# Four of twelve query units ahead of a loop with a run-time trip count, in a one-core graph, attention and experts kernel

## The chip, the cores and the metric

The kernel runs as one program on one core of a Trainium2 chip. The metric is the device time of one execution in microseconds (us). The time before is the median of three runs, 812.83 us, with 811.21 us the lowest and 817.26 us the highest. The profile is of a fourth execution.

## The reference, cut to what matters

```python
xn = layernorm(x)                      # 1250 nodes x 512
x = x + gnn(xn, edges) + mix(xn)       # this stage
x = x + ffn(layernorm(x))              # shared and routed experts, later

# gnn: mean over the incoming edges (40000 edges, sorted by target)
agg = segment_sum(xn[src], dst) / max(count, 1)
h = relu(layernorm(xn @ w_self.T + agg @ w_neigh.T + bias))

# mix: linear attention, 8 heads of 64
phi(t) = elu(t @ proj) + 1
kv = phi(k).T @ v;  z = 1 / (phi(q) @ phi(k).sum(0))
out = (phi(q) @ kv * z) @ w_proj + b_proj
```

The change touches phi(q) and the mean over the edges. With the projection folded into the weights, phi of a value u is relu(u) + exp(-relu(-u)): two Relu's and one Exp on ScalarE, and one addition on VectorE.

## The kernel before, in words

Nodes are held in ten tiles of 125. Every engine has its order of work written out by hand, and all hand over through semaphores. Around the change the order is this.

**Ahead of the loop.** VectorE makes one-hot matrices of the edges, TensorE multiplies them into counts (L1284), ScalarE copies the counts out (L490), and TensorE multiplies them with the normalized rows (`spread`, L1291). Nine of the ten blocks of nodes are done so at fixed places, with the key and value products (L1228) and their sum over nodes (`kvacc`, L1309) between them. The last of these on TensorE are `spread`, `degrees` and `kvacc(9)`. ScalarE ends this part with `aggregate_out(8)` (L497).

**The loop.** What is left is done in a loop whose trip count is read at run time from `tab` by each engine (`value_load`, L1370 on TensorE). For this data it is passed once: five one-hot pairs on VectorE (L812, L815), 40 count matmuls (L1284), three copies on ScalarE (L540), 20 matmuls of `spread` (L1291) and ten of L1379, which set `x_mm`. Four of the five one-hot pairs are made before TensorE comes to the loop; the fifth waits for TensorE's first count in it.

**The means.** VectorE adds the loop's result (L911), inverts the counts and scales the ten blocks of `aggacc` (L920, each sets `an_rdy`). `means_T(b)` then turns block b: four transposes on TensorE (L1387) into bank 6 or 7, a copy to 16 bit on ScalarE (L545, `aT_h`) and the low part on VectorE (L924, `aT_rdy`), which frees the bank for block b + 2.

**The query units.** There are twelve, in order n = 0 to 11: eight of 500 nodes and four of 250. Unit n is 12 matmuls on TensorE (`split3`, L1228, called from L1397) into a bank `qb[n % 4]`, then Relu, Relu, Exp on ScalarE (L558, L559, L561) into a place of `mscr`, then the addition into `qphi` on VectorE (L935, `q_rdy`). There are two places, so ScalarE's unit n waits for `q_rdy` of unit n - 2. `qphi` lies over `aggacc`, so no addition can be made before all means are turned; on VectorE all ten low parts stand ahead of the first addition. On TensorE the means are laid between the units by `MEANS`: 0, 1, 2 after unit 0; 3, 4, 5 after unit 1; 6, 7 after unit 2; 8, 9 after unit 3. On ScalarE means 0 to 2 stand after unit 0 and 3 to 9 after unit 1. Units 4 and later wait on TensorE for the Relu's of unit n - 4 (`q_rel`).

**Among them** `unit(1)` and `unit(2)` convert weights from `stg` to `W`: one activation on ScalarE (L427) and one operation on VectorE (L714, `w_rdy`). They stand after query units 4 and 8 on both engines. SyncE loads weight unit u into `stg` when `w_rdy` has reached u - 1 (L267, L268). VectorE also copies the key-value sums into `kvbd` after its second addition (L946, L947).

**The attention.** Over ten tiles t: `att(t)` on TensorE (L1413), which needs `q_rdy` of the group, `kvbd` and, for t = 0 and 1, the Relu's of the last units (`q_rel` 10 and 12, L1409); reciprocals and products on VectorE (L955, L962), behind the last addition in VectorE's order; `att_turn(t)` (L1422); a copy on ScalarE (L571); the low part (L968); `project(t)` (L1228); and the addition to x (L974). Six more weight units are converted in the same stretch. Everything after it (graph layer, expert layers, output) has no change.

Of the kernel before, what the change touches and what calls it, by code (L numbers as in the profile page):

```python
# [10 lines left out]
ALU = mybir.AluOpType  # L11
ACT = mybir.ActivationFunctionType
# [6 lines left out]
HD = DIM // HEADS  # L19
# [3 lines left out]
P = 125  # L23
TILES = NODES // P
C = DIM // 128
J = HID // 128
PAIRS = HEADS // 2
ETILES = EDGES // P
BLK = 125
NBLK = NODES // BLK  # L30
# [16 lines left out]
WS = 256.0  # L47
# [1 line left out]
NSLOT = 8  # L49
NSTG = 2  # L50
GROUPS = [(0, 4), (4, 4), (8, 2)]
MEANS = [(0, 1, 2), (3, 4, 5), (6, 7), (8, 9)] + [()] * 8
PARTS = [(0, 112), (112, P)]

U_V, U_PROJ, U_SELF, U_NEIGH = 0, 1, 2, 3
# [24 lines left out]
def build(nc, a, out):  # L80
    with ExitStack() as ctx:
# [7 lines left out]
        ps = [PS[:, i, :] for i in range(8)]  # L89
# [5 lines left out]
        xT = sb("xT", [128, 2, C, NODES], F16)  # L95
# [134 lines left out]
        block = ctx.enter_context(nc.Block())  # L230

        kvb = [ps[3], ps[5]]
        qb = [ps[0], ps[1], ps[2], ps[4]]
        turned = [PS[:, 2 * z:2 * z + 2, :].rearrange("p b (j n) -> p (b j) n", n=ST) for z in range(2)]

        sobank = [ps[i] for i in (5, 6, 7, 0, 1, 2, 3, 4)]
# [180 lines left out]
        def _(act):  # L417
            s = nc.scalar

            def unit(u):  # L420
                act.wait_ge(stg_in[u % NSTG], 16 * (u // NSTG + 1))
                what = unit_needs(u)
                if what and what[0] == "expert":
                    act.wait_ge(S["me_mm"], ends[what[1]] + 1)
                elif what:
                    act.wait_ge(S[what[0]], what[1])
                s.activation(W[:, u % NSLOT, 0, :], stg[:, u % NSTG, :], ACT.Copy, scale=WS).then_inc(S["w_h"], 1)  # L427
# [103 lines left out]
                    value_out((g - G0) // 4)  # L531
            aggregate_out(FIX - 1)

            act.wait_ge(S["tab_rdy"], 1)
            items = act.value_load(tab[0:1, 2 * ITEMS:2 * ITEMS + 1], min_val=1, max_val=ITEMS)
            with act.Fori(0, items) as i:
# [3 lines left out]
                    s.activation(CT[0][:, :, 2 * SUB * q:2 * SUB * q + SUB * n],  # L540
                                 ps[q][:, 0:n * KEYS].rearrange("p (d t) -> p t d", t=TILES), ACT.Copy).then_inc(S["x_ct"], 1)

            def means_T(b):
                act.wait_ge(S["aT_mm"], b + 1)
                s.activation(aggT[:, 0, :, b * BLK:(b + 1) * BLK], ps[6 + b % 2][:, 0:C * BLK].rearrange("p (c n) -> p c n", c=C),  # L545
                             ACT.Copy).then_inc(S["aT_h"], 1)


            n = 0
            for t0, nt in GROUPS:  # L550
                for r in range(PAIRS):
                    o, w = 1024 * (n % 2), nt * P
                    act.wait_ge(S["q_mm"], n + 1)
                    if n >= 2:
                        act.wait_ge(S["q_rdy"], n - 1)
                    else:
                        act.wait_ge(S["k_rdy"], TILES)
                    s.activation(mscr[:, o:o + w], qb[n % 4][:, 0:w], ACT.Relu, scale=-1 / WS).then_inc(S["q_neg"], 1)  # L558
                    s.activation(mscr[:, o + 512:o + 512 + w], qb[n % 4][:, 0:w], ACT.Relu, scale=1 / WS).then_inc(S["q_rel"], 1)  # L559
                    act.wait_ge(S["q_neg"], n + 1)  # L560
                    s.activation(mscr[:, o:o + w], mscr[:, o:o + w], ACT.Exp, scale=-1.0).then_inc(S["q_exp"], 1)  # L561
                    for b in (range(3), range(3, NBLK))[n] if n < 2 else ():
                        means_T(b)
                    if n in (4, 8):
                        unit(n // 4)
                    n += 1
            for t in range(TILES):
                act.wait_ge(S["tT_mm"], t + 1)
                if t >= 2:
# [82 lines left out]
            n = 0  # L652
# [49 lines left out]
        def _(dve):  # L702
# [9 lines left out]
            def unit(u):  # L712
                dve.wait_ge(S["w_h"], u + 1)
                v.scalar_tensor_tensor(out=W[:, u % NSLOT, 1, :], in0=stg[:, u % NSTG, :], scalar=WS,  # L714
                                       in1=W[:, u % NSLOT, 0, :], op0=ALU.mult, op1=ALU.subtract).then_inc(S["w_rdy"], 1)
# [211 lines left out]

            for b in range(NBLK):
                means_T(b)
            n = 0  # L930
            for t0, nt in GROUPS:
                for r in range(PAIRS):
                    o, w = 1024 * (n % 2), nt * P
                    dve.wait_ge(S["q_exp"], n + 1)
                    v.scalar_tensor_tensor(out=qphi[:, r, t0 * P:t0 * P + w], in0=mscr[:, o:o + w], scalar=1.0,  # L935
                                           in1=mscr[:, o + 512:o + 512 + w], op0=ALU.mult, op1=ALU.add).then_inc(S["q_rdy"], 1)
                    n += 1
                    if n in (5, 9):
                        unit(n // 4)
                    if n == 2:  # L940
                        dve.wait_ge(S["kvacc_mm"], TILES)
                        for z in range(2):
                            kv2 = kvb[z][:, 0:258].rearrange("p (r n) -> p r n", r=2)
                            for h in range(2):
                                q = slice(HD * h, HD * h + HD)
                                v.tensor_copy(kvbd[q, 2 * z:2 * z + 2, HD * h:HD * h + HD], kv2[q, :, HD * h:HD * h + HD]).then_inc(S["kvbd_rdy"], 1)  # L946
                                v.tensor_copy(kvbd[q, 2 * z:2 * z + 2, 128 + h:129 + h], kv2[q, :, 128:129]).then_inc(S["kvbd_rdy"], 1)  # L947

            def att(t):
                for z in range(2):  # L950
# [270 lines left out]
        def _(pe):  # L1221
            te = nc.tensor

            def split3(dst, lhs, rhs, n, first, last, between=None):

                for c in range(n):
                    for k, (sl, sr) in enumerate(((0, 0), (0, 1), (1, 0))):
                        ins = te.matmul(dst, lhs(sl, c), rhs(sr, c), start=(first and c == 0 and k == 0),  # L1228
                                        stop=(last and c == n - 1 and k == 2))
                        if between is not None:  # L1230
                            between(3 * c + k)
                return ins
# [132 lines left out]
            degrees(FIX - 1)  # L1365
            kvacc(TILES - 1)

            pe.wait_ge(S["tab_rdy"], 1)
            pe.wait_ge(S["agg_ev"], FIX)
            items = pe.value_load(tab[0:1, 2 * ITEMS:2 * ITEMS + 1], min_val=1, max_val=ITEMS)  # L1370
# [11 lines left out]
            def means_T(b):  # L1382
                pe.wait_ge(S["an_rdy"], b + 1)
                if b >= 2:
                    pe.wait_ge(S["aT_rdy"], b - 1)
                for c in range(C):
                    ins = te.transpose(ps[6 + b % 2][:, c * BLK:(c + 1) * BLK], aggacc[0:BLK, b, c * 128:(c + 1) * 128], ident[0:BLK, 0:BLK])  # L1387
                ins.then_inc(S["aT_mm"], 1)


            pe.wait_ge(S["wp_rdy"], 8)
            n = 0
            for t0, nt in GROUPS:
                for r in range(PAIRS):
                    if n >= 4:
                        pe.wait_ge(S["q_rel"], n - 3)
                    split3(qb[n % 4][:, 0:nt * P], lambda s, c: Wqp[:, s, 0, c, r * 128:(r + 1) * 128],  # L1397
                           lambda s, c: xT[:, s, c, t0 * P:(t0 + nt) * P], C, True, True).then_inc(S["q_mm"], 1)
                    for b in MEANS[n]:
                        means_T(b)  # L1400
                    n += 1
            pe.wait_ge(S["kvbd_rdy"], 8)

            def att(t):
# [225 lines left out]
```

## Time and profile before

| | |
|---|---|
| median of three runs | 812.83 us (811.21 to 817.26) |
| the profiled execution | 814.13 us |
| its span | 812.3 us |
| around the span | 1.8 us |
| TensorE matmuls | 732.5 us busy, 90% of the span |
| VectorE | 423.0 us, 52% |
| ScalarE | 271.3 us, 33% |
| GpSimdE | 220.4 us, 27% |
| mean granted TensorE clock | 0.968 |

PE is the matmuls of TensorE, PEld its weight loads, DVE is VectorE, ACT ScalarE, POOL GpSimdE, SP SyncE. Times in rows are microseconds from the start of the span, and L1228 is line 1228 of the kernel before. The granted clock is 1.00 at 2.4 GHz and 0.50 at 1.2 GHz. The ends of matmuls in the records are modelled, so a group's length is longer than the distance to the next group by a tenth or two of a microsecond; distances from start to start are used where they matter.

### The profile page before, as it was taken

How to read it: one execution, taken by the hardware profiler on the slowest of the kernel's cores; microseconds unless marked ns; L12 is line 12 of the kernel's file. 1: busy time of each engine (PE TensorE's matmuls, PEld its weight loads, DVE VectorE, ACT ScalarE, POOL GpSimd, SP SyncE). 2: the span in 40 equal slices, each digit the busy share in tenths (PEclk: the TensorE clock that was granted, in tenths of full speed). 3: DMA queues.
4: the chain of work that ended last, by engine and by line, in shares of the span. 5: the costliest groups of instructions: out<-in, count | busy, mean ns of one | idle time of the engine just before them, and what ended most of it. 6: DMA issues, size and time to landing. Idle time of an engine off the chain costs nothing.

```text
span 812.3 us, 11827 instructions
## 1 busy us (share of the span) xinstructions
PE 732.5 (90%) x4148; PEld 452.3 (56%) x4148; DVE 423.0 (52%) x797; ACT 271.3 (33%) x396; POOL 220.4 (27%) x211
## 2 busy tenths in 40 slices
PE   0735999999979898999899999999969999999998
PEld 0613577777646764565566664444745555555554
DVE  6579776576845894369643542222234634321153
ACT  2741223233237540122653322333344544422000
POOL 4397132142100000000222223444532222211372
PEclk9965999999999999999999999999979999999999
DMA  9120100000001460000013331111138785443574
GB/s 249 30 101 1 52 1 1 1 1 1 1 1 48 147 246 1 1 1 0 26 52 103 106 100 26 52 53 53 53 101 309 261 314 183 167 132 127 176 201 134
DMA packets 24224, 73.36 MB, mean 90 GB/s; under 512 B 7122, under 2 KB 7468, under 8 KB 20209
## 3 DMA queue, kind: packets, MB, share of 16 engines
q1 hardware_dynamic: 9233, 40.13, 14.7%
q0 software_dynamic: 10624, 24.99, 10.5%
q10 hardware_dynamic: 4320, 7.62, 2.5%
q8 instruction: 29, 0.48, 0.2%
q14 instruction: 18, 0.15, 0.1%
HBM read 57.38 MB, written 15.31 MB: 89 GB/s over the span
## 4 chain that ended last, share of the span: by engine, by line
PE 73%; DVE 10%; ACT 6%; DMA 4%; issue 3%; POOL 2%; SPq 1%; ACTq 0%; DVEq 0%
PE banks L1228 56%; PE banks L1291 5%; PE banks L1284 5%; DMA y_rows<-xT 2%; DMA big<-in_proj_mat 2%; PE banks L1539 2%; POOL W L325 1%; ACT W L427 1%; PE banks L1309 1%; DVE st L735 1%; DVE W L714 1%; PE banks L1413 1%; DMA stg<-in_units 1%; ACT big L585 1%; ACT xT L681 1%
## 5 line engine op out<-in xcount | busy, mean ns | idle before, releaser
L1228 PE MATMUL banks<-W,xT 128*125 128x512 f16 (+1 forms) x1392 | 319.4, 384 | 3.7 <-ACT xT L681 1.9
L1228 PEld LDWEIGHTS banks<-W,xT 128*125 128x125 f16 (+1 forms) x1392 | 166.5, 122 | 133.8 <-issue 13.8
L1228 PE MATMUL banks<-xT,W 128*128 128x500 f16 (+1 forms) x720 | 128.1, 339 | 1.8 <-DVE xn L1180 1.4
L1228 PEld LDWEIGHTS banks<-xT,W 128*128 128x128 f16 x720 | 69.8, 97 | 58.3 <-DVE xn L1180 1.6
L358 POOL TENSOR_TENSOR big<-xn,big 125x512 f16<-125x512 f32 x20 | 23.4, 1171 | 247.5 <-ACT big L600 247.5
L714 DVE SCALAR_TENSOR_TENSOR W<-stg,W 128x2048 f16<-128x2048 f32 x30 | 68.1, 2289 | 35.5 <-ACT W L427 35.4
L1228 PE MATMUL banks<-W,big 128*125 128x512 f16 x360 | 81.5, 380 | 0.0
L369 POOL DMA_INDIRECT xn<-h_rows,tokidx x28 | 34.7, 1240 | 125.1 <-PE banks L1539 111.5
L1198 DVE CAST xT<-banks 128x1024 f32 x23 | 28.1, 1221 | 72.9 <-PE banks L1539 72.9
L1228 PEld LDWEIGHTS banks<-W,big 128*125 128x125 f16 x360 | 48.3, 136 | 29.2 <-issue 2.3
L427 ACT ACTIVATE W<-stg 128x2048 f16<-128x2048 f32 x30 | 56.4, 1903 | 6.5 <-DMA stg<-in_units 6.5
L1291 PE MATMUL banks<-W,big 125*125 125x512 f16 x200 | 51.0, 385 | 1.3 <-ACT big L497 0.8
L1180 DVE SCALAR_TENSOR_TENSOR xn<-banks,xn 128x500 f32<-128x500 f32 (+1 forms) x24 | 14.2, 590 | 69.8 <-ACT xn L660 67.8
L344 POOL TENSOR_TENSOR W<-big 125x625 f16<-125x625 f16 x9 | 16.0, 1775 | 103.6 <-ACT big L490 103.6
L1284 PE MATMUL banks<-W 125*128 125x250 f16 x208 | 30.6, 294 | 9.3 <-DVE W L815 7.3
L681 ACT ACTIVATE xT<-banks 128x512 f32<-128x512 f32 x24 | 14.3, 597 | 70.4 <-PE banks L1228 54.1
L382 POOL TENSOR_TENSOR big<-xn,big 128x500 f16<-128x500 f32 (+1 forms) x24 | 22.6, 942 | 48.7 <-ACT big L663 48.6
L812 DVE TENSOR_TENSOR W<-big 125x2000 f16<-125x2000 f16 x26 | 32.8, 1263 | 1.5 <-DVE big L807 1.4
L1291 PEld LDWEIGHTS banks<-W,big 125*125 125x125 f16 x200 | 26.1, 137 | 13.1 <-issue 2.9
L1228 PE MATMUL banks<-W,xn 128*125 128x512 f16 x120 | 29.2, 394 | 3.5 <-DVE xn L968 3.5
L1539 PE MATMUL banks<-ident,xn 128*128 128x128 f16 x384 | 26.9, 223 | 5.1 <-issue 3.2
L1050 DVE SCALAR_TENSOR_TENSOR xn<-banks,xn 125x512 f32<-125x512 f32 x20 | 13.8, 689 | 33.7 <-ACT xn L596 33.6
(284 smaller groups left out, 886.9 us busy)
## 6 DMA issues: line engine op xcount, KB each, us to landing
stg<-in_units SPq DMA_DIRECT2D x30, 1024.0 KB, 5.3
y_rows<-xT ACTq DMA_DIRECT2D x29, 256.0 KB, 3.7
h_rows<-big POOLq DMA_DIRECT2D x10, 500.0 KB, 3.6
out_x<-x SPq DMA_DIRECT2D x10, 224.0 KB
stg<-in_wqkT SPq DMA_DIRECT2D x1, 2048.0 KB, 17.5
x<-in_x SPq DMA_DIRECT2D x2, 896.0 KB
x<-in_x SPq DMA_DIRECT2D x1, 448.0 KB
xn<-h_rows,tokidx POOLq DMA_INDIRECT x28, 5.0
```

The lines of the kernel that those rows point to most:

```text
L358: g.tensor_tensor(hrow[t % 2][:, HID + 512 * u:HID + 512 * (u + 1)], mscr[0:P, 1024 + 512 * u:1536 + 512 * u], hrow[t % 2][:, 512 * u:512 ...
L369: g.indirect_dma_start(hg[i % 2], None, h_rows, bass.IndirectOffsetOnAxis(ap=tokidx[:, i:i + 1], axis=0)).then_inc(g_in[i % 2], 16)
L382: g.tensor_tensor(hT[:, 1, j, c0:c0 + w], mscr[:, 1024 + 512 * (n % 2):1024 + 512 * (n % 2) + w], hT[:, 0, j, c0:c0 + w], ALU.subtract).th ...
L427: s.activation(W[:, u % NSLOT, 0, :], stg[:, u % NSTG, :], ACT.Copy, scale=WS).then_inc(S["w_h"], 1)
L681: s.activation(yb, ps[4][:, :], ACT.Copy).then_inc(S["y_cp"], 1)
L714: v.scalar_tensor_tensor(out=W[:, u % NSLOT, 1, :], in0=stg[:, u % NSTG, :], scalar=WS, in1=W[:, u % NSLOT, 0, :], op0=ALU.mult, op1=ALU.s ...
L812: v.tensor_tensor(oht[z % RING], iotaK.unsqueeze(1).to_broadcast(wide), krel[k].rearrange("p (a b) -> p a b", b=2).unsqueeze(2).to_broadca ...
L1198: v.tensor_copy(hgT[:, bass.ds((i + 1) % 2, 1), 1].rearrange("p z j n -> p (z j) n"), turned[1]).then_inc(S["hg_l"], 1)
L1228: ins = te.matmul(dst, lhs(sl, c), rhs(sr, c), start=(first and c == 0 and k == 0), stop=(last and c == n - 1 and k == 2))
L1284: ins = te.matmul(ps[q][:, h * KEYS:(h + 1) * KEYS], ohp[z][:, a, :, b], oht[z][:, a, :, b], start=(a == 0 and b == 0), stop=(a == CH // 2 ...
L1291: ins = te.matmul(ps[4][0:BLK, :], CT[z][0:P, t, :], xs[:, s, t, :], start=(t == 0 and s == 0), stop=(t == TILES - 1 and s == 1))
L1539: ins = te.matmul(turned[s][:, j, :], rows(s * HID + j * 128), ident16[:, :], start=True, stop=True)
```

## The change

Units 0 to 3 (500 nodes each) move ahead of the loop on TensorE, right behind `kvacc(9)`, and on ScalarE, right behind `aggregate_out(8)`. They alternate between banks 6 and 7, since banks 0 to 5 belong to the loop and to the key-value sums. `mscr` gets four places, so that their results can lie there over the loop. VectorE's additions stay behind the means. The means stand among units 4 to 7 on TensorE, and on ScalarE all ten stand ahead of unit 4. ScalarE's unit n waits for `q_rdy` of unit n - 4. The weight conversions stand after units 5 and 9 on ScalarE and after additions 6 and 10 on VectorE; the copies into `kvbd` come after the fourth addition.

```diff
-MEANS = [(0, 1, 2), (3, 4, 5), (6, 7), (8, 9)] + [()] * 8
+MEANS = [()] * 4 + [(0, 1, 2), (3, 4, 5), (6, 7), (8, 9)] + [()] * 4
+QLEAD = 4
+QUNITS = [(t0, nt, r) for t0, nt in GROUPS for r in range(PAIRS)]
...
-        qb = [ps[0], ps[1], ps[2], ps[4]]
+        qb = [ps[6], ps[7], ps[6], ps[7]] + 2 * [ps[0], ps[1], ps[2], ps[4]]
...
+            def query_phi(n):
+                o, w = 1024 * (n % 4), QUNITS[n][1] * P
+                act.wait_ge(S["q_mm"], n + 1)
+                if n == 0:
+                    act.wait_ge(S["kvacc_mm"], TILES)
+                if n >= 4:
+                    act.wait_ge(S["q_rdy"], n - 3)
+                s.activation(mscr[:, o:o + w], qb[n][:, 0:w], ACT.Relu, scale=-1 / WS).then_inc(S["q_neg"], 1)
+                s.activation(mscr[:, o + 512:o + 512 + w], qb[n][:, 0:w], ACT.Relu, scale=1 / WS).then_inc(S["q_rel"], 1)
+                act.wait_ge(S["q_neg"], n + 1)
+                s.activation(mscr[:, o:o + w], mscr[:, o:o + w], ACT.Exp, scale=-1.0).then_inc(S["q_exp"], 1)
+
+            for n in range(QLEAD):
+                query_phi(n)
+
             act.wait_ge(S["tab_rdy"], 1)
...
+            for b in range(NBLK):
+                means_T(b)
+            for n in range(QLEAD, 3 * PAIRS):
+                query_phi(n)
+                if n in (5, 9):
+                    unit(n // 4)
...
+            for n in range(3 * PAIRS):
+                (t0, nt, r), o = QUNITS[n], 1024 * (n % 4)
+                w = nt * P
+                dve.wait_ge(S["q_exp"], n + 1)
+                v.scalar_tensor_tensor(out=qphi[:, r, t0 * P:t0 * P + w], in0=mscr[:, o:o + w], scalar=1.0,
+                                       in1=mscr[:, o + 512:o + 512 + w], op0=ALU.mult, op1=ALU.add).then_inc(S["q_rdy"], 1)
+                if n in (6, 10):
+                    unit(n // 4)
+                if n == 3:
+                    dve.wait_ge(S["kvacc_mm"], TILES)
...
+            def query_mm(n):
+                t0, nt, r = QUNITS[n]
+                if n == 0:
+                    pe.wait_ge(S["wp_rdy"], 8)
+                    pe.wait_ge(S["k_rel"], TILES)
+                if n == 1:
+                    pe.wait_ge(S["v_ev"], TILES)
+                if n in (2, 3):
+                    pe.wait_ge(S["q_rel"], n - 1)
+                if n >= 8:
+                    pe.wait_ge(S["q_rel"], n - 3)
+                split3(qb[n][:, 0:nt * P], lambda s, c: Wqp[:, s, 0, c, r * 128:(r + 1) * 128],
+                       lambda s, c: xT[:, s, c, t0 * P:(t0 + nt) * P], C, True, True).then_inc(S["q_mm"], 1)
+
+            for n in range(QLEAD):
+                query_mm(n)
             pe.wait_ge(S["tab_rdy"], 1)
             pe.wait_ge(S["agg_ev"], FIX)
...
+            for n in range(QLEAD, 3 * PAIRS):
+                query_mm(n)
+                for b in MEANS[n]:
+                    means_T(b)
             pe.wait_ge(S["kvbd_rdy"], 8)
```

## Rows read from the trace of the kernel before

**Rows 1.** The page, part 4: the chain that ended last, by engine
```profile
PE 73%; DVE 10%; ACT 6%; DMA 4%; issue 3%; POOL 2%; SPq 1%; ACTq 0%; DVEq 0%
```

**Rows 2.** The same chain in order of time, 205 to 310: start, length, what
```profile
218.13 0.84 issue
218.97 4.73 PE banks L1284 x40
...
228.76 0.54 PE banks L1379 x10
...
231.07 4.05 DVE big L920 x10
...
265.07 2.29 DVE W L714
```

**Rows 3.** The timeline of PE: start, length, line, operation, count, idle time before it
```profile
229.15 2.69 PE L1228 MATMUL banks<-xT,W 128*128 128x500 f16 x12
...
238.84 1.02 PE L1387 MATMUL banks<-ident,big 125*128 125x125 f32 x8
241.95 0.62 PE L1387 MATMUL banks<-ident,big 125*128 125x125 f32 x4 [2.09 <-DVE big L924]
...
245.80 2.70 PE L1228 MATMUL banks<-xT,W 128*128 128x500 f16 x12
248.33 1.02 PE L1387 MATMUL banks<-ident,big 125*128 125x125 f32 x8
249.19 15.41 PE L1228 MATMUL banks<-xT,W 128*128 128x500 f16 x96
...
268.48 2.00 PE L1413 MATMUL banks<-kvbd,big 128*125 128x130 f32 x8 [1.64 <-ACT xn L559]
270.27 1.06 PE L1422 MATMUL banks<-ident,xn 125*128 125x125 f32 x4
```

**Rows 4.** The timeline of ACT
```profile
217.16 0.60 ACT L497 ACTIVATE big<-banks 125x512 f32<-125x512 f32 x1 [4.68 <-PE banks L1291]
...
251.53 0.59 ACT L558 ACTIVATE xn<-banks 128x500 f32<-128x500 f32 x1 [1.50 <-DVE big L935]
...
255.88 1.94 ACT L427 ACTIVATE W<-stg 128x2048 f16<-128x2048 f32 x1
257.68 0.62 ACT L558 ACTIVATE xn<-banks 128x500 f32<-128x500 f32 x1
...
262.29 0.38 ACT L558 ACTIVATE xn<-banks 128x250 f32<-128x250 f32 x1
...
263.10 1.93 ACT L427 ACTIVATE W<-stg 128x2048 f16<-128x2048 f32 x1
...
267.78 0.38 ACT L558 ACTIVATE xn<-banks 128x250 f32<-128x250 f32 x1 [1.07 <-DVE big L935]
```

**Rows 5.** The timeline of DVE
```profile
241.12 1.27 DVE L924 TENSOR_TENSOR big<-banks,big 128x500 f16<-128x500 f32 x2 [3.31 <-ACT big L545]
...
249.59 1.26 DVE L924 TENSOR_TENSOR big<-banks,big 128x500 f16<-128x500 f32 x2 [2.13 <-ACT big L545]
250.77 1.26 DVE L935 SCALAR_TENSOR_TENSOR big<-xn 128x500 f32<-128x500 f32 x2
...
267.27 0.74 DVE L935 SCALAR_TENSOR_TENSOR big<-xn 128x250 f32<-128x250 f32 x2
...
269.21 0.25 DVE L955 RECIPROCAL rs<-banks 125x4 f32<-125x4 f32 x2
```

**Rows 6.** Windows of 1 us: busy PE, PEld, DVE, ACT, POOL (count), PEclk, DMA share, GB/s
```profile
267.00:268.00 1.00, 0.00 (x0) 0.00 (x0) 1.00 (x3) 0.22 (x1) 0.00 (x0) 1.00 0.32 123
...
269.00:270.00 1.00, 1.00 (x6) 1.00 (x6) 0.97 (x5) 0.00 (x0) 0.00 (x0) 0.50 0.87 301
```

**Rows 7.** The timeline of SP, 200 to 305: issue of weight loads 4 to 10
```profile
267.38 33.22 SPq L268 DMA_DIRECT2D stg<-in_units  x7
```

**Rows 8.** The page, part 6: size and median time from issue to landing
```profile
stg<-in_units SPq DMA_DIRECT2D x30, 1024.0 KB, 5.3
```

More of the change, by code:

```diff
@@ L532, in _, with means_T @@
             aggregate_out(FIX - 1)
+            def means_T(b):
+                act.wait_ge(S["aT_mm"], b + 1)
+                s.activation(aggT[:, 0, :, b * BLK:(b + 1) * BLK], ps[6 + b % 2][:, 0:C * BLK].rearrange("p (c n) -> p c n", c=C),
+                             ACT.Copy).then_inc(S["aT_h"], 1)
+            def query_phi(n):
[11 more added lines that the diff above has]
+                query_phi(n)
             act.wait_ge(S["tab_rdy"], 1)
@@ L541, in _ @@
                                  ps[q][:, 0:n * KEYS].rearrange("p (d t) -> p t d", t=TILES), ACT.Copy).then_inc(S["x_ct"], 1)
[L543 to L566, printed above, removed]
+            for b in range(NBLK):
[4 more added lines that the diff above has]
+                    unit(n // 4)
             for t in range(TILES):
@@ L929, in _ @@
                 means_T(b)
[L930 to L947, printed above, removed]
+            for n in range(3 * PAIRS):
[8 more added lines that the diff above has]
+                    dve.wait_ge(S["kvacc_mm"], TILES)
+                    for z in range(2):
+                        kv2 = kvb[z][:, 0:258].rearrange("p (r n) -> p r n", r=2)
+                        for h in range(2):
+                            q = slice(HD * h, HD * h + HD)
+                            v.tensor_copy(kvbd[q, 2 * z:2 * z + 2, HD * h:HD * h + HD], kv2[q, :, HD * h:HD * h + HD]).then_inc(S["kvbd_rdy"], 1)
+                            v.tensor_copy(kvbd[q, 2 * z:2 * z + 2, 128 + h:129 + h], kv2[q, :, 128:129]).then_inc(S["kvbd_rdy"], 1)
             def att(t):
@@ L1388, in means_T @@
                 ins.then_inc(S["aT_mm"], 1)
[L1391 to L1401, printed above, removed]
+            for n in range(QLEAD, 3 * PAIRS):
+                query_mm(n)
+                for b in MEANS[n]:
+                    means_T(b)
             pe.wait_ge(S["kvbd_rdy"], 8)
```

## The prediction

> **What bounds the kernel now.** I read the chain of waits first. TensorE holds 73% of it over the whole span, VectorE 10%, ScalarE 6% [rows 1]. That speaks for a kernel in which time is won by closing TensorE's gaps, and in which matmuls that are merely moved cost nothing. Whether that holds in the stretch of the change is to be read from the same chain in order of time. From the loop to the end of the means it does run on TensorE, with two calls at VectorE and ScalarE. But behind the means it leaves TensorE: VectorE's weight conversion at 265.07 is on it [rows 2], and TensorE's second `att` waits for ScalarE's Relu's at 268.48 [rows 3]. So there are two parts with different limits. Up to the means TensorE's work is exposed. From the means to the attention, the third view, the timelines of ScalarE and VectorE, decides: ScalarE starts its third query unit at 251.53, when VectorE has made its first addition, and works its queue down until its last unit starts at 267.78; VectorE comes to the reciprocals of the attention at 269.21 [rows 4, 5]. TensorE has eight query units in that time and is done with them at 264.6 (249.19 and 15.41) [rows 3], 3.9 us before the `att` that waits. Four of these units are what the change takes out, so to speak, to put as many ahead of the loop: the cover is left, and exposed time is entered.
>
> **Step 1, the lead on TensorE.** `kvacc(9)` ends at 218.13 and the loop's first matmul is at 218.97, after 0.84 of "issue" [rows 2]. One unit of 500 nodes takes 2.53 from start to start (245.80 to 248.33) [rows 3], so four take 10.1. I looked for waits in them. Units 0 and 1 need keys, values and weights that are long there. Unit 2 needs bank 6, which ScalarE frees some 1.1 after unit 0 ends (its two Relu's, within a whole unit's 1.45, below), well inside the 2.53 of unit 1. So the four run without a gap, 218.13 to 228.25. VectorE has nothing more to do ahead of TensorE's first count, so it doesn't gain by the time: its fifth pair of one-hots still waits for that count. ScalarE ends the Exp of unit 3 some 1.6 after 228.25, at 229.9, when two counts of the loop are about through; it can be late for the loop's first copy by about 1, but not for the third, on which `spread` waits. The loop is as long as before.
>
> What becomes of the 0.84? ScalarE's last copy ends at 217.76 [rows 4], and TensorE's first count comes 1.2 later; that is the reading of the trip count behind the wait. With 10 us of matmuls ahead of it and the wait long fulfilled, it can be read while they run. Bounds: 0 to 0.84 left. I take 0.1, since where TensorE leaves the loop its next unit starts at 229.15 with no gap behind the ten small matmuls (229.30 is their end) [rows 2, 3]. So the loop moves by 10.1 - 0.84 + 0.1 = **+9.4** (9.3 to 10.1): it ends at 238.7 in place of 229.30.
>
> The trace agrees with a rule of the Trainium skill as far as it goes ("TensorE: Matmul & The Clock Gate", section "Architectural detail"): TensorE has a queue of 64 instructions between sequencer and array. Four units are 96 instructions, so by it the sequencer would be past them well before the array is, and the whole 0.84 would vanish: +9.3 in place of +9.4. No row here shows a register read behind a full queue.
>
> **Step 2, the means.** They lie among units 4 to 7 as they lay among 0 to 3, units of the same width. The first gap of TensorE there is set by VectorE, which scales all ten blocks (4.05) before its first low part [rows 2]; it stays. The second gap, 2.09 ahead of the transposes of mean 5 [rows 3], came because ScalarE had query unit 1 ahead of means 3 and 4. VectorE's low parts began 2.28 after that pair's transposes (238.84 to 241.12); for means 8 and 9, where ScalarE is free, it is 1.26 (248.33 to 249.59) [rows 3, 5]. Now ScalarE has nothing but means, so **-1.0**. The other pairs don't wait. VectorE's first addition was at 250.77 [rows 5] and comes at 250.77 + 9.4 - 1.0 = 259.2. ScalarE's unit 4 waits for it (same place of `mscr` as unit 0) and follows 0.76 later as before (250.77 to 251.53): at **259.9**.
>
> **Step 3, ScalarE behind the means.** A wide unit takes 1.45 (three in 251.53 to 255.88), a conversion 1.80 (255.88 to 257.68), a narrow unit 0.81 (262.29 to 263.10) [rows 4]. Before, ten units and two conversions went from 251.53 to the start of the last at 267.78, 16.25, with a wait of 1.07 for a place in it [rows 4]. After: four wide, a conversion, two narrow, a conversion, one narrow, then the last: 5.80 + 1.80 + 1.62 + 1.80 + 0.81 = 11.83. With four places no wait for VectorE is left, as I follow it: addition 7 is done at 269.7, unit 11 needs it at 271.7. So the last unit starts at 271.7, 4.4 less than the shift. TensorE must give units 8 to 11 in time: unit 8 may start when the Relu's of unit 4 are done, 261.0, and a narrow unit takes 1.3 ((15.4 - 10.1) / 4) [rows 3]; unit 10 waits for the Relu's of unit 6 and ends at 267.0, four microseconds before ScalarE comes to it.
>
> **Step 4, VectorE's tail.** Here something new is late. The second conversion stood behind addition 8; now it stands behind addition 10, with only addition 11 behind it. From the start of ScalarE's last unit to the reciprocals it was 1.43 (267.78 to 269.21), 0.37 of it an addition (0.74 for two) [rows 4, 5], so an addition starts about 1.0 after its unit. Unit 10 starts at 270.9, its addition ends at 272.3, the conversion takes 2.20 (265.07 to 267.27) [rows 2, 5], addition 11 another 0.4: the reciprocals of `att(0)` come at **274.9** in place of 269.21, **+5.7**. The two `att` of TensorE are at 272.4 at the latest (0.70 after ScalarE's last unit, as 267.78 to 268.48), so they are early. The eight small copies into `kvbd` move from behind addition 1 to behind addition 3 and are done near 263; nobody waits for them.
>
> **Step 5, behind it.** The transposes of `att_turn(0)` follow the reciprocals by 1.06 as before (269.21 to 270.27) [rows 3, 5], and the rest of the attention hangs on them. Its weight loads shift too: load 4 was issued at 267.38, 1.8 before the reciprocals [rows 7], and is issued at 274.5 now, 0.4 before them; with 5.3 to landing [rows 8] it is there at 279.8. ScalarE wants it some 8 us behind the reciprocals, so it is in time. From there the order and the durations are the old ones, and I know of no slack that takes back a uniform shift. VectorE no longer waits for `att(1)`: worth 0 to 0.9; TensorE's clock may cost 0 to 3 (below); I set the two against each other, at nothing.
>
> **The sum** against the profiled execution: 814.13 + 9.4 - 1.0 - 2.7 (16.25 and 1.43 against 11.83 and 3.2) = 819.8. That execution lies 1.3 above the median of the runs, so on the median's scale the forecast is 812.83 + 5.7 = **818.5 us**, 0.7% slower.
>
> **The rivals.**
>
> *TensorE decides (a win).* If the stretch behind the means were bound by TensorE, moving units would be free, and only closed gaps would count: 0.7 ahead of the loop, 1.0 in the means, 1.6 ahead of the second `att`: 3.3 less, 809.5 us. For it speaks TensorE's 73% of the chain [rows 1]. Against it: TensorE stood still at 267 for a whole microsecond while VectorE converted [rows 6]. It decides only if ScalarE's and VectorE's 15 us behind the means fall below TensorE's four narrow units, 5.2. Chance 0.1.
>
> *The clock falls.* Before, TensorE's clock went from 1.00 (2.4 GHz) to 0.50 (1.2 GHz) at 269, after two pauses around one `att` [rows 6]. After the change it has only 5.2 us of units between the end of the means (257.8) and 276, with a pause of 3.2 at the start. At half the clock the narrow units take 2.6 each and end at 271.4, still ahead of the reciprocals; but `att_turn(0)` starts the dense work cold, and one or two `project` (2.5 each, like a unit) take double. Before, the clock was low at that place too, and VectorE's conversions follow ScalarE more than `project`. Price 0 to 4 over the forecast, 821.5 us with 3 of them. Chance 0.2. The skill's rule (same page, "Part 1: The HAM clock gate"), that throttled is the default state and activity lifts it, points the same way.
>
> *The shift is partly taken back.* The attention's later tiles wait for weight loads; if their rhythm is less tied to the start than I hold, 3 us come back: 815.5 us. Against: each load waits for a conversion in this very chain. Chance 0.08.
>
> *The lead units don't run ahead,* because a wait holds TensorE ahead of the loop (a bank, a late Relu): each microsecond of it is exposed, 819.5 to 822 us. The waits found are fulfilled by over 1 us. Chance 0.04. My forecast keeps 0.58.
>
> **How the numbers follow.** This kernel's measurement can tell about 1% (8.1 us) from no change. Slower by more begins at 821.0: most of the clock's case and some of the forecast's own spread (the conversion, the gap, 1 to 2 us of runs that themselves lay from 811.2 to 817.3) give 0.27. Faster by over 1% needs under 804.7, more than the winning rival gives: 0.04. Within 1%: 0.69. The range takes in the winning rival at its full price and the clock to nearly 5: 809 to 823.5 us; the forecast's own is 816 to 821.
>
> **What would show it.** Right: 48 matmuls between `kvacc` and the loop without a gap, to about 228.3; the loop's end at 238 to 239.5; no second gap of 2 us in the means, one of about 1; TensorE idle about 3 us behind the last mean; VectorE's second conversion directly ahead of the last addition, at 272 to 275, and on the chain; the reciprocals at 274 to 276. Wrong: a reading of the trip count that costs more than 0.84; a stall at unit 2 or 3; ScalarE waiting for places; or a stretch from the reciprocals to the graph layer that is shorter than before by more than 1 us.

## The result, and the profile after

The changed kernel takes **822.18 us**, the median of six runs (821.65 to 828.53), against 812.63 us before (six runs, 811.21 to 817.26): the ratio is 1.0131, with a 95% interval of 1.0100 to 1.0161. It is slower, as forecast (818.5), and by 9.5 us where 5.7 were forecast. A ratio here is computed from all the runs and can lie up to 0.4% from the quotient of the two medians.

The profiled execution took 822.32 us with a span of 820.5, 8.2 over the span before. The chain of waits of it, in order of time (start, length, what), answers to [rows 2]:

```profile
216.25 1.00 PE banks L1312 x8
217.25 10.13 PE banks L1231 x48
227.38 4.56 PE banks L1287 x40
...
237.00 0.54 PE banks L1398 x10
...
239.31 4.05 DVE big L925 x10
...
272.29 0.42 DVE big L939
272.71 0.45 DVE W L719
273.16 1.67 issue
274.83 0.42 DVE big L939
```

The 0.84 of "issue" between `kvacc` and the loop is gone to the last tenth: the lead's 48 matmuls end at 227.38 and the first count begins there. Behind the means the chain runs along ScalarE's queue from 260.18 on, passes to VectorE at 272.29, and has VectorE's second conversion ahead of the last addition. Line numbers differ from the kernel before: L1231 is `split3`, L1287 the counts, L1312 `kvacc`, L1398 the ten small matmuls at the loop's end, L1406 the means' transposes, L929 VectorE's low parts, L939 the addition, L719 its conversion. On ScalarE L548, L549 and L551 are Relu, Relu and Exp.

The timeline of TensorE of the same kernel, to compare with [rows 3]:

```profile
239.92 1.02 PE L1406 MATMUL banks<-ident,big 125*128 125x125 f32 x8
244.10 1.06 PE L1406 MATMUL banks<-ident,big 125*128 125x125 f32 x4 [3.16 <-DVE big L929]
244.95 3.74 PE L1231 MATMUL banks<-xT,W 128*128 128x500 f16 x12
248.53 1.02 PE L1406 MATMUL banks<-ident,big 125*128 125x125 f32 x8
250.60 0.62 PE L1406 MATMUL banks<-ident,big 125*128 125x125 f32 x4 [1.06 <-DVE big L929]
...
261.30 4.09 PE L1231 MATMUL banks<-xT,W 128*128 128x250 f16 x24 [3.31 <-ACT xn L549]
...
279.76 3.46 PE L1231 MATMUL banks<-W,xn 128*125 128x512 f16 x12
```

The second pause of the means is 1.06 in place of 2.09, and TensorE waits 3.31 for ScalarE behind the means, both as forecast. But the unit at 244.95 takes 3.74 in place of 2.7, and the first `project`, at 279.76, 3.46. The windows of 1 us (busy PE, PEld, DVE, ACT, POOL, then the granted clock, DMA share, GB/s) say why:

```profile
242.00:243.00 1.00, 0.00 (x0) 0.00 (x0) 1.00 (x4) 0.00 (x0) 0.00 (x0) 1.00 0.00 0
245.00:246.00 1.00, 1.00 (x4) 0.41 (x3) 0.17 (x1) 0.59 (x1) 0.00 (x0) 0.50 0.00 0
262.00:263.00 1.00, 1.00 (x7) 0.71 (x6) 0.91 (x7) 1.00 (x3) 0.00 (x0) 0.50 0.00 0
279.00:280.00 1.00, 1.00 (x6) 0.98 (x5) 0.83 (x4) 0.00 (x1) 0.00 (x0) 0.50 1.03 377
```

TensorE's clock is at 1.2 GHz three times between the loop and the first `project`: from 243.6, in the pause of 3.16 in the means, from 260.7, ahead of the narrow units, and from 274.4, behind the second `att`, to 281.2, in the first `project`. In the kernel before, the same pause (3.15) left the clock at 1.00.

VectorE's timeline, for [rows 5]:

```profile
259.42 2.44 DVE L939 SCALAR_TENSOR_TENSOR big<-xn 128x500 f32<-128x500 f32 x4
...
272.29 0.42 DVE L939 SCALAR_TENSOR_TENSOR big<-xn 128x250 f32<-128x250 f32 x1 [1.65 <-ACT xn L551]
272.62 2.28 DVE L719 SCALAR_TENSOR_TENSOR W<-stg,W 128x2048 f16<-128x2048 f32 x1
274.83 0.41 DVE L939 SCALAR_TENSOR_TENSOR big<-xn 128x250 f32<-128x250 f32 x1
275.27 0.25 DVE L958 RECIPROCAL rs<-banks 125x4 f32<-125x4 f32 x2
```

**Where the time is.** The parts ahead of the change scatter from profile to profile, so I measure each kernel's marks from the end of its own `kvacc` (217.25 here, 218.13 before). The marks are the end of the loop, the first addition, the first reciprocal, the first `project` and the graph layer's first copy (L577 before). The last column is the time from that copy to the end of the span.

```text
                      loop   first     first    first    graph   rest of
                      end    addition  recipr.  project  layer   the span
before               11.16    32.64     51.08    54.76   103.77   490.4
the change           20.28    42.17     58.02    62.51   111.81   491.4
```

The difference of 8.0 at the graph layer is 9.12 (lead) + 0.41 (means) - 2.59 (ScalarE and VectorE behind them) + 0.81 (to the first `project`) + 0.29 (rest of the attention). The forecast had 9.4, -1.0, -2.7, 0 and 0. Outside this stretch 0.9 were won ahead of `kvacc` and 1.0 lost behind the graph layer's first copy, where nothing was changed. Nearly all of it lies in one place: from the first to the second result of the loop of the routed experts it takes 8.9 us in place of 8.0, with the clock at 0.50 up to 619.1, where the kernel before has it back at 610.0. The kernel before has one profile, so its column carries no scatter of its own.

### The profile page after: what moved, and what is told of

It is laid out like the page before. It is cut to its first block, busy times and chain, and to the rows that moved or that the text cites. A ratio compares the mean times of both kernels' runs of the same rounds, so it can differ in the third digit from the quotient of the medians.

```text
span 820.5 us, 11825 instructions
## 1 busy us (share of the span) xinstructions
PE 738.2 (90%) x4148; PEld 454.8 (55%) x4148; DVE 422.4 (51%) x797; ACT 271.6 (33%) x396; POOL 219.5 (27%) x211
## 4 chain that ended last, share of the span: by engine, by line
PE 73%; DVE 10%; ACT 6%; DMA 4%; issue 3%; POOL 2%; SPq 1%; DVEq 0%; ACTq 0%
PE banks L1231 56%; PE banks L1294 5%; PE banks L1287 5%; PE banks L1551 2%; ACT W L429 2%; DMA big<-in_proj_mat 2%; POOL W L327 1%; DMA y_rows<-xT 1%; DMA stg<-in_units 1%; PE banks L1312 1%; DVE st L740 1%; DVE W L719 1%; ACT big L590 1%; SPq L259 1%; ACT xn L551 0%
## 5 line engine op out<-in xcount | busy, mean ns | idle before, releaser
L1231 PE MATMUL banks<-W,xT 128*125 128x512 f16 (+1 forms) x1392 | 320.2, 384 | 3.8 <-ACT xT L686 2.0
L1231 PEld LDWEIGHTS banks<-W,xT 128*125 128x125 f16 (+1 forms) x1392 | 166.7, 122 | 134.3 <-issue 14.9
L1231 PE MATMUL banks<-xT,W 128*128 128x500 f16 (+1 forms) x720 | 131.0, 343 | 5.8 <-ACT xn L549 3.9
L1231 PEld LDWEIGHTS banks<-xT,W 128*128 128x128 f16 x720 | 70.6, 99 | 64.2 <-ACT xn L549 4.7
L719 DVE SCALAR_TENSOR_TENSOR W<-stg,W 128x2048 f16<-128x2048 f32 x30 | 68.1, 2289 | 33.6 <-ACT W L429 33.6
L1231 PE MATMUL banks<-W,big 128*125 128x512 f16 x360 | 81.5, 380 | 0.0
L1231 PEld LDWEIGHTS banks<-W,big 128*125 128x125 f16 x360 | 48.3, 136 | 29.2 <-issue 2.3
L1287 PE MATMUL banks<-W 125*128 125x250 f16 x208 | 30.7, 295 | 8.6 <-DVE W L820 7.5
L686 ACT ACTIVATE xT<-banks 128x512 f32<-128x512 f32 x24 | 14.3, 597 | 70.8 <-PE banks L1231 50.6
L384 POOL TENSOR_TENSOR big<-xn,big 128x500 f16<-128x500 f32 (+1 forms) x24 | 22.6, 943 | 48.8 <-ACT big L668 48.7
L1231 PE MATMUL banks<-W,xn 128*125 128x512 f16 x120 | 30.1, 404 | 3.5 <-DVE xn L971 3.5
```

What stands on the lines that cost most here:

```text
L384: g.tensor_tensor(hT[:, 1, j, c0:c0 + w], mscr[:, 1024 + 512 * (n % 2):1024 + 512 * (n % 2) + w], hT[:, 0, j, c0:c0 + w], ALU.subtract).th ...
L1287: ins = te.matmul(ps[q][:, h * KEYS:(h + 1) * KEYS], ohp[z][:, a, :, b], oht[z][:, a, :, b], start=(a == 0 and b == 0), stop=(a == CH // 2 ...
```

## The experiments

The theory to be tested: the lead's work is exposed where it now lies; what it saves behind the means is only ScalarE's time; and the miss of 2.3 us is TensorE's clock. In these kernels the orders behind the loop are written as lists: q is a query unit, m a mean, u a weight conversion; [a..b] is a run of them. Each has the median of ten runs (the control and the run of 804.61 us, four), beside runs of the kernel before in the same call with medians of 812.9, 812.9 and 813.6.

**No unit ahead, all else kept.**

```diff
-QLEAD = 4
+QLEAD = 0
-qb = [ps[6], ps[7], ps[6], ps[7]] + 2 * [ps[0], ps[1], ps[2], ps[4]]
+qb = 3 * [ps[0], ps[1], ps[2], ps[4]]
-TensorE  q4 m012 q5 m345 q6 m67 q7 m89 q[8..11]
+TensorE  q0 m012 q1 m345 q2 m67 q3 m89 q[4..11]
-ScalarE  m[0..9] q4 q5 u1 q[6..9] u2 q10 q11
+ScalarE  q0 m012 q1 m[3..9] q[2..5] u1 q[6..9] u2 q10 q11
```

> No unit ahead of the loop; all other edits of the change stay (four places, conversions after units 5 and 9 and additions 6 and 10, kvbd copies after addition 3), the means stand among units 0 to 3. Theory (TensorE's work ahead of the loop is exposed, behind the means ScalarE and VectorE decide): the 9.3 us of the lead are gone and the four places take ScalarE's waits out; TensorE's units end at 264.6 as before, the reciprocals come near 268.0: 811.4 us, 1.2 under the kernel before. Rival (the loss lies in the places or in the moved conversions): 818 us or more.

Measured: 813.13 us, ratio 0.9962 (0.9919 to 1.0006), so not told apart from the kernel before; the runs go from 810.8 to 818.8. The loss lies in the lead and not in the places or the conversions: the rival falls. The profiled execution is the longest of the ten, 818.84. Its first addition is at 37.16, 4.5 later than before, because two units of the means ran with the clock at 0.50; another 2.1 of its length lie ahead of `kvacc`. TensorE's timeline:

```profile
237.94 1.07 PE L1404 MATMUL banks<-ident,big 125*128 125x125 f32 x4 [3.16 <-DVE big L928]
238.81 5.13 PE L1230 MATMUL banks<-xT,W 128*128 128x500 f16 x12
243.77 1.02 PE L1404 MATMUL banks<-ident,big 125*128 125x125 f32 x8
246.88 0.83 PE L1404 MATMUL banks<-ident,big 125*128 125x125 f32 x4 [2.09 <-DVE big L928]
247.50 4.21 PE L1230 MATMUL banks<-xT,W 128*128 128x500 f16 x12
```

The same pause, before the same transposes, costs nothing in one execution and starts a loss of 4.5 us in another. Nine of the 75 executions of the kernel before took 817.1 to 818.3 with a mean clock of 0.960, against 0.963 to 0.968 in those under 815; that the clock fell there in the same way is likely, but none of them was profiled. Taking the 4.5 off, the reciprocals would be at 50.6 against 51.1 before: 0.5 earlier, where 1.2 were expected.

**Two units ahead.**

```diff
-QLEAD = 4
+QLEAD = 2
-qb = [ps[6], ps[7], ps[6], ps[7]] + 2 * [ps[0], ps[1], ps[2], ps[4]]
+qb = [ps[6], ps[7], ps[2], ps[4]] + 2 * [ps[0], ps[1], ps[2], ps[4]]
-TensorE  q4 m012 q5 m345 q6 m67 q7 m89 q[8..11]
+TensorE  q2 m012 q3 m345 q4 m67 q5 m89 q[6..11]
-ScalarE  m[0..9] q4 q5 u1 ...
+ScalarE  q2 m012 q3 m[3..9] q4 q5 u1 ...
```

> Two units ahead of the loop, the rest as in the change. Theory: the loop moves by 4.2; units 2 and 3 are done by ScalarE among the means as units 0 and 1 were before, so ScalarE has as little behind the means as with four ahead (last unit 11.8 us after its first): reciprocals at 270.8, 1.6 later than before, and TensorE has six units behind the means, so its clock does not fall there: 814.2 us. Rival (each moved unit costs its own 2.5 us and nothing is regained): 816.8 us. Rival (moving is free): 812.6.

Measured: 819.37 us, ratio 1.0052 (1.0007 to 1.0098), the fastest of its runs 817.29. The forecast of 814.2 is missed; the time lies above both rivals too, and the one at 816.8 is the nearest. The profile has the clock down in the means here too (units of 4.38 and 4.26). The lead moves the end of the loop by 4.06, and the first addition comes 3.35 behind where this alone would put it (40.05 against 32.64 + 4.06). To tell the work from the clock, the next kernel keeps the clock up.

**Two units ahead, TensorE kept busy in the first pause of the means.** The extra matmuls write a bank that a later unit overwrites.

```diff
-TensorE  q2 m0 m1 m2 q3 ...
+TensorE  q2 m0 m1 (12 extra matmuls) m2 q3 ...
```

> Two units ahead of the loop as in the earlier run, with 12 extra matmuls (results unused) in TensorE's first pause of the means. Theory (two units ahead cost 1.6 us by their work, and the rest of the 819.4 measured was TensorE's clock, which fell in that pause and had to be made up by 3.4 us, and again at the att): the clock stays up in the means, 3 us under the run without the extra matmuls: 816 us. Rival (each moved unit simply costs its 2.5 us): no change, 819.

Measured: 816.65 us, 2.7 under the run without the extra matmuls; ratio 1.0043 (1.0018 to 1.0068). TensorE's timeline:

```profile
234.89 2.69 PE L1410 MATMUL banks<-xT,W 128*128 128x500 f16 x12
238.21 0.62 PE L1404 MATMUL banks<-ident,big 125*128 125x125 f32 x4 [0.63 <-DVE big L928]
238.67 2.70 PE L1230 MATMUL banks<-xT,W 128*128 128x500 f16 x12
...
244.76 2.70 PE L1230 MATMUL banks<-xT,W 128*128 128x500 f16 x12
...
266.54 2.01 PE L1430 MATMUL banks<-kvbd,big 128*125 128x130 f32 x8 [2.22 <-ACT xn L552]
```

The units (L1230) are back at 2.70; L1410 are the extra matmuls. The first addition is at 36.69 (32.64 + 4.06 = 36.70), the reciprocals at 52.54, 1.5 behind the kernel before where 1.6 were expected. So the work of two units costs 1.5, and the clock cost 3.4 in the means. The graph layer is at 107.25, 3.5 over before, so 2.0 more come behind the reciprocals: 0.8 up to the first `project`, and 1.2 between it and the graph layer. There the clock is low in the kernel before from 313.0 to 316.4 and in this run from 311.0 to 317.9. That this causes the 1.2 was not tested by an edit.

**The change, TensorE kept busy in its long pauses.** Run twice. The 8 extra matmuls behind the means wait until mean 8 has freed their bank.

```diff
-TensorE  q4 m0 m1 m2 ... m8 m9 q8 ...; att(0) att(1) att_turn(0)
+TensorE  q4 m0 m1 (12 extra) m2 ... m8 m9 (8 extra) q8 ...; att(0) (9 extra) att(1) (9 extra) att_turn(0)
```

> The change with extra matmuls (results unused) in TensorE's pauses: 12 ahead of mean 2, 8 behind mean 9, 9 after each of the first two att. Theory (2.4 us of the loss are TensorE's clock: it fell to 1.2 GHz in the pause of the means, which cost 1.3, and stood there again at the first project, 1.1): the clock stays at 1.00 from 240 to 285 and the time is 2.4 us under the change: 819.8. Rival (the low clock lies in time that ScalarE and VectorE decide): 822.2, no change.

Measured: 821.70 us, ratio 1.0086 (1.0046 to 1.0125). In the profile the clock stays at 1.00 from `kvacc` to 316.5, and the first addition and the first `project` are where the work puts them:

```profile
246.04 2.70 PE L1230 MATMUL banks<-xT,W 128*128 128x500 f16 x12
...
278.39 2.80 PE L1230 MATMUL banks<-W,xn 128*125 128x512 f16 x12
```

First addition 40.73 (the change 42.17), reciprocals 56.59 (58.02), `project` 59.65 (62.51), graph layer 108.27 (111.81). That is 1.4 in the means and 1.4 more at the first `project`, near the 1.3 and 1.1 of the theory. Yet the time is only 0.5 less than the change's.

> The change with the extra matmuls in TensorE's pauses, once more. In the first such run the profile had the stretch from kvacc to the graph layer 3.5 us shorter than the change's, but the whole was only 0.5 shorter: 1.5 us were lost ahead of kvacc and 2 in the loop of the routed experts, where nothing was edited. Theory (those are scatter of that execution): this profile again has the stretch 3.5 shorter, and other times in the other two parts. Rival (something that belongs to this kernel, such as where its instructions lie, costs them): the same losses again, 821 to 822 us.

Measured: 822.44 us, ratio 1.0090 (1.0052 to 1.0128). The marks up to the first `project` repeat to 0.02. The graph layer doesn't: it is at 110.03, 1.8 behind the first run of this kernel and only 1.8 ahead of the change, where 3.5 were expected. Between the first `project` and that mark the clock was low from 313.3 to 320.1, in the first run from 316.5 to 319.9. The part ahead of `kvacc` went from 218.74 to 215.61: that is scatter. But the loop of the routed experts is long again: from its first to its last result 149.4 and 151.3 us, against 146.3 to 147.5 in the eleven other profiles. What is longer are single passes, in which ScalarE waits for the store of `y_rows` to land and TensorE waits for ScalarE. Timelines of ScalarE and TensorE:

```profile
631.87 0.60 ACT L685 ACTIVATE xT<-banks 128x512 f32<-128x512 f32 x1 [5.48 <-DMA y_rows<-xT]
632.65 1.68 PE L1230 MATMUL banks<-W,xT 128*128 128x512 f16 x7 [1.62 <-ACT xT L685]
```

TensorE waits so three times in this profile (1.62, 1.55, 1.77) and once in the first (1.41); behind the first pass no other profile has a wait of TensorE over 0.4 in this loop. The share of these stores in the chain of waits is no sign of it by itself: 22.6% of the loop here and 3.9% in the control, but 12.3% in the first run of this kernel and 11.7% in the kernel before, whose loop is among the shortest. The rival of this run holds for the loop, in two profiles of two: something that goes with this kernel costs 2 to 5 us there. What makes the stores late was not found. So this pair of runs shows the clock's share up to the first `project`, and doesn't show it in the total.

**The control: the change once more.**

> The changed kernel once more, as control of the others of this call: 821 to 823 us by every theory. In its profile TensorE's clock should again fall in the first pause of the means or just behind it and again around the first att; if it stays up in the means, the excess over the forecast there (1.3 us) should be gone in this execution.

Measured: 822.16 us, ratio 1.0116 (1.0096 to 1.0135). All marks repeat to 0.06, and the clock falls at the same places. So in this kernel the fall in the means is hardly chance. Whether it goes with where the pause lies is not shown: in the run with no unit ahead the pause lay in the same place as in the kernel before, and the clock fell in one and not in the other.

**The conversions ahead, among the means.**

```diff
-ScalarE  m[0..9] q4 q5 u1 q[6..9] u2 q10 q11
+ScalarE  m0 m1 u1 m[2..5] u2 m[6..9] q[4..11]
-VectorE  m[0..9] q[0..3] kvbd q4 q5 q6 u1 q[7..10] u2 q11
+VectorE  m0 m1 u1 m[2..5] u2 m[6..9] q[0..3] kvbd q[4..11]
```

> The change with the two weight conversions moved ahead: unit(1) behind mean 1 and unit(2) behind mean 5, on ScalarE and VectorE. Theory (behind the means ScalarE's and VectorE's queues decide): ScalarE has 3.6 us less behind the means and VectorE no conversion ahead of addition 11; reciprocals 9.7 us after ScalarE's unit 4 in place of 15.1: 5.4 us under the change, 816.8. Rival (TensorE or the weight loads decide): within 1 us of the change, 821 to 823.

Measured: 814.17 us, 8.0 under the change; ratio 0.9983 (0.9943 to 1.0023) to the kernel before. The reciprocals are at 52.67, 5.35 earlier (5.4 expected), and the clock is up again for the first `project`, which comes 6.8 earlier. ScalarE and VectorE decide behind the means; the rival falls. VectorE's timeline shows an unbroken row of additions, each waiting 0.42 for ScalarE:

```profile
267.67 0.42 DVE L936 SCALAR_TENSOR_TENSOR big<-xn 128x250 f32<-128x250 f32 x1 [0.42 <-ACT xn L554]
268.50 0.42 DVE L936 SCALAR_TENSOR_TENSOR big<-xn 128x250 f32<-128x250 f32 x1 [0.42 <-ACT xn L554]
268.96 0.25 DVE L957 RECIPROCAL rs<-banks 125x4 f32<-125x4 f32 x2
```

**The second conversion alone, two additions earlier.**

```diff
-ScalarE  ... q[6..9] u2 q10 q11
+ScalarE  ... q[6..8] u2 q9 q10 q11
-VectorE  ... q[7..10] u2 q11
+VectorE  ... q7 q8 u2 q9 q10 q11
```

> The change with the second weight conversion one unit earlier on ScalarE (behind unit 8) and two additions earlier on VectorE (behind addition 8). Theory (step 4 of the prediction: VectorE's conversion directly ahead of addition 11 holds up the reciprocals): the reciprocals come 1.3 us earlier, 13.7 behind ScalarE's unit 4 in place of 15.1; 820.8 us. Rival (ScalarE's last unit decides by itself): no change, 822.2.

Measured: 821.66 us, ratio 1.0083 (1.0046 to 1.0120); the total can't tell 1 us. In the profile the reciprocals are at 56.92, 1.1 earlier and 14.5 behind the first addition in place of 15.85. The step is right in its place and, at 1.35 counted from the first addition (1.3 expected), in its size.

**No lead, a unit between each two means, conversions among the means.**

```diff
+QLEAD = 0, qb = 3 * [ps[0], ps[1], ps[2], ps[4]]
+TensorE  q0 m01 q1 m23 q2 m45 q3 m67 q4 m89 q[5..11]
+ScalarE  q0 m01 u1 q1 m23 q2 m45 u2 m67 q3 m89 q[4..11]
+VectorE  m0 m1 u1 m[2..5] u2 m[6..9] q[0..3] kvbd q[4..11]
```

> No unit ahead of the loop, four places; on TensorE one unit stands between each two means (units 0 to 4), on ScalarE and VectorE the two weight conversions stand behind means 1 and 5, ScalarE does units 0 to 3 among the means. Theory: TensorE has no pause left in the means, the means end 3.6 us earlier, and behind them ScalarE and VectorE have so little that TensorE decides (its units end 30.7 us behind the loop); reciprocals 7.6 us earlier than before: 805 us, and up to 1 less for the clock. Rival (the means' chain through three engines decides as before): 810 or more.

Measured: **804.61 us**, ratio 0.9905 (0.9885 to 0.9924): faster than both kernels, by 8.2 us than the one before. TensorE's pauses in the means are two of 0.62, and its last seven units follow without a gap:

```profile
233.94 1.20 PE L1404 MATMUL banks<-ident,big 125*128 125x125 f32 x8 [0.62 <-DVE big L928]
...
246.14 12.88 PE L1230 MATMUL banks<-xT,W 128*128 128x500 f16 x84
258.86 2.06 PE L1421 MATMUL banks<-kvbd,big 128*125 128x130 f32 x16
```

The reciprocals are at 44.29, 6.8 earlier than before (7.6 expected), and the graph layer is 9.1 earlier. The difference is 0.6 at the first `project` and 1.7 between it and the graph layer: in this profile the clock is at 1.00 the whole time from `kvacc` to 587.2, and the low stretch that the kernel before has at 313.0 to 316.4 is missing. So about 2 of the 8.2 go with the clock, and the rest is the order.

**The same with four units ahead.**

```diff
+QLEAD = 4
+TensorE  q4 m01 q5 m23 q6 m45 q7 m67 m89 q[8..11]
+ScalarE  m0 m1 u1 m[2..5] u2 m[6..9] q[4..11]
```

> As the run with a unit between each two means, but with four units ahead of the loop as in the change, and the other eight behind it. Theory (work ahead of the loop is exposed, and behind the means ScalarE and VectorE decide again when TensorE has only four narrow units left): reciprocals 2.2 us earlier than in the kernel before: 810.5 us, 5 above the run without the lead. Rival (moving is free where TensorE decides): equal to that run, 805.

Measured: 812.96 us, ratio 1.0002 (0.9989 to 1.0015). It loses 8.4 against the run without the lead (5 expected); the reciprocals are 6.3 later (50.63), and only 0.5 ahead of the kernel before, where 2.2 were expected. TensorE has its pauses back, since nothing is left to fill them:

```profile
252.79 1.20 PE L1404 MATMUL banks<-ident,big 125*128 125x125 f32 x8 [2.15 <-DVE big L928]
257.14 7.84 PE L1230 MATMUL banks<-xT,W 128*128 128x250 f16 x48 [3.15 <-ACT xn L552]
```

The 48 narrow matmuls take 7.84, where 5.2 would do at full clock, so up to 2.6 of the 6.3 are the clock and the rest is the lead. "Moving is free" is refuted where it had its best chance.

**No lead, a unit between the means, conversions where the change has them.**

```diff
-ScalarE  q0 m01 u1 q1 m23 q2 m45 u2 m67 q3 m89 q[4..11]
+ScalarE  q0 m01 q1 m23 q2 m45 m67 q3 m89 q4 q5 u1 q[6..9] u2 q10 q11
-VectorE  m0 m1 u1 m[2..5] u2 ...
+VectorE  m[0..9] q[0..3] kvbd q4 q5 q6 u1 q[7..10] u2 q11
```

> The run with no lead and a unit between each two means, but with the weight conversions left where the change has them (behind units 5 and 9, additions 6 and 10). Theory (filled pauses and early means give the first part of that run's gain, the conversions the rest): the first addition comes as early as there, 31.4 behind kvacc, the reciprocals 15.8 later at 47.2, against 51.1 before and 44.3 there: 808.9 us. Rival (the gain is all from the conversions): 812.

Measured: 811.56 us, ratio 0.9943 (0.9901 to 0.9984). By the total the rival (812) is nearer than the theory (808.9); the marks tell the two apart. The first addition is at 30.52 and the reciprocals at 46.38, 4.7 earlier than before; but only 2.8 of it are left at the graph layer (100.97), with the clock down at the `att` again, from 262.8 to 269.7, and once more from 307.2 to 310.6. So both edits bring something, and the conversions' place pays twice: 2.1 at the reciprocals and 4.2 more behind them, in this pair of profiles.

## Why the prediction was right, and where it was short

**Direction and mechanism: right.** The chain's 73% on TensorE was not the answer; its order in time was. Units moved ahead of the loop are exposed (+9.12 against 9.4), and what their leaving saves behind the means is ScalarE's and VectorE's (-2.59 against -2.7). Taking the lead out (813.1), shortening it (two units: 1.5 us of work) and moving the conversions (-8.0) agree.

**Step 1: right.** No gap at units 2 and 3, and the gap of 0.84 vanished whole; I had left 0.1. From `kvacc` to the first count it is 10.13, the four units and nothing else (four times 2.53). The Trainium skill ("TensorE: Matmul & The Clock Gate", section "Architectural detail") gives TensorE's queue a depth of 64 instructions; this trace, with 96 instructions ahead of the count and no gap, agrees. The loop's end, forecast for 238 to 239.5 on the clock of the profile, came at 237.5, because `kvacc` itself was 0.9 earlier in this execution; counted from `kvacc` it fits.

**Step 2: the term was mis-sized.** The second pause shrank by the 1.03 read from [rows 3, 5]; but the step let the rest lie "as they lay among 0 to 3", and TensorE's clock fell in the first pause. Forecast -1.0, measured +0.41, 1.44 of it the clock, by the run with extra matmuls (40.73 against 42.17).

**Steps 3 and 4: right.** ScalarE's last unit starts 11.86 after its unit 4 (11.83 in the forecast). From the first addition to the reciprocals 15.85 against 15.7 in the forecast; TensorE's idle time 3.31 against 3.2; the second conversion on the chain at 272.62. The run with that conversion alone earlier gave 1.1 back.

**Step 5: the term was mis-sized.** "I set the two against each other, at nothing": VectorE's freedom from `att(1)` against the clock, 0 to 3. In the change `project` follows the reciprocals by 4.49, with the clock up by 3.06 and in the kernel before by 3.68. So the clock costs 1.4 in all and 0.8 more than before. What VectorE's freedom from `att(1)` is worth was not measured apart from it. The rival "the clock falls" (821.5 us, chance 0.2) named the case that came, and the rows before did show its signs: two pauses around one `att` with the clock down at 269 [rows 6]. That its time lies so near the measured one is partly luck: it put 3 us at `att_turn(0)` and the first `project`, where the runs show 0.8, and nothing in the means, where they show 1.4.

**The rest.** Forecast 5.7, measured 8.0 in the stretch; 1.4 in the means, 0.8 at `project` and 0.3 behind make up 2.5, another 0.1 is from the stretch behind the means, and 0.3 less from the lead. The median difference of 9.5 is 1.5 more. Of this, 1.0 stands behind the graph layer in both profiles of the change (491.4 and 491.3, against 490.4 before), at the first pass of the experts' loop. The part ahead of `kvacc` differs by up to 4.6 from profile to profile, and what of the rest is its doing stays open.

**The rivals.** TensorE decides: refuted, also in the version where it truly decides without a lead (804.6 against 813.0 with one). Lead units that don't run ahead: refuted by the chain. A shift that is taken back behind the reciprocals: refuted, it grew from 6.9 there to 8.0 at the graph layer. One reading against the first rival was too broad: in the window 267 to 268 of [rows 6] VectorE's conversion is over at 267.36, and the rest is additions.

## What to carry to other kernels

A unit of work on the engine with the longest chain is free to move only where another engine decides the end; read the chain in order of time on both sides of the move, not its sum. Units that can be placed freely are best spent in that engine's pauses: the four units that cost 9 us of TensorE's time ahead of the loop are part of an order that gains 8 when units fill the pauses and the conversions stand among the means. And small fixed work (here two conversions) belongs where its engines wait, not in the queue that the next stage waits for.

## What the runs showed of the hardware

TensorE's clock is a cost to be counted at each pause. A pause of 3.15 to 3.16 ahead of the same transposes left the granted clock at 1.00 in the profile before. In the change it fell to 0.50 in this pause (1.4 us). With two units ahead (3.4) and in a run with none (4.5) it fell around this pause too, and once more around the next one, of 2.09. In two profiles of the changed kernel it fell at the same places. The Trainium skill ("TensorE: Matmul & The Clock Gate", "Part 1: The HAM clock gate") says that activity lifts the throttle and idleness restores it. The traces agree, and in them one and the same pause goes either way.

Not expected either: a kernel with only 38 more matmuls, all before the graph layer, twice had its loop of the routed experts 2 to 5 us longer, in passes where TensorE waited 1.4 to 1.8 behind a late store of `y_rows`. Why they were late stays open.
